# Ends of the expert stage in a fused Mamba and mixture-of-experts kernel: norms, splits and output groups in another order

## The reference

```python
def _layernorm(x, axis=-1, eps=1e-05):
    m = jnp.mean(x, axis=axis, keepdims=True)
    v = jnp.var(x, axis=axis, keepdims=True)
    return (x - m) / jnp.sqrt(v + eps)

# block 1: a Mamba block (norm, input projection, causal convolution of 4 taps, silu,
# step sizes by softplus, state scan over 1024 steps with 256 x 64 states, gate, projection)
x = _layernorm(x + mamba(x))

# block 2: four layers, each a mixture of 4 experts, the best 2 of 4 weighted
def _moe_layer(x, rw, rb, g, b, w1, b1, w2, b2):
    probs = softmax(x @ rw + rb); vals, idx = top_k(probs, 2); vals = vals / vals.sum()
    xhat = (x - mean) * rsqrt(var + EPS)
    xe = xhat[None] * g + b                      # per expert
    h = gelu(xe @ w1 + b1)                       # 128 -> 512, per expert
    y = h @ w2 + b2                              # 512 -> 128
    return sum over experts of comb * (x + y)    # comb: vals, zero for the two others
y = x
for l in range(4): y = _moe_layer(y, ...)
x = _layernorm(x + y)
```

## Time and profile before

| | |
|---|---|
| median of 3 runs | 2267.18 us |
| lowest, highest | 2264.71, 2272.36 us |
| the profiled execution, its own time | 2264.66 us |
| its span | 2262.8 us |
| PE, DVE, ACT, POOL busy | 95%, 81%, 71%, 42% of the span |
| expert stage | about 1386 to 2258 us of the span |

### The profile page before, as it was taken

The page is one execution under the profiler, slowest core; times in us unless marked ns, Lnnn a source line. Parts: engine busy times, 40 slices in busy tenths (PEclk is TensorE's granted clock), DMA queues, the critical chain, the costliest instruction groups (busy, mean ns, idle before and its releaser), DMA issues. The chain is left out here.

```text
span 2262.8 us, 50361 instructions
## 1 busy us (share of the span) xinstructions
PE 2139.4 (95%) x16960; PEld 1260.6 (56%) x16960; DVE 1841.2 (81%) x2779; ACT 1598.0 (71%) x2070; POOL 944.1 (42%) x452
## 2 busy tenths in 40 slices
PE   7887999999999999999999997999999999999997
PEld 3342333333333333333333335899999999999986
DVE  5768999999999999999999997565565566556665
ACT  4677988888888888888888884555455455544543
POOL 3225343434444443434343443544444444444442
PEclk9895999999999999999999999999999999999999
DMA  5887222222221212122221225100100010000000
GB/s 166 249 242 190 44 45 44 46 41 45 42 46 39 46 39 46 39 49 42 46 45 41 47 47 149 38 0 0 38 1 0 0 38 1 0 1 1 10 10 18
DMA packets 354957, 114.93 MB, mean 51 GB/s; under 512 B 283000, under 2 KB 345600, under 8 KB 354624
## 3 DMA queue, kind: packets, MB, share of 16 engines
q1 hardware_dynamic: 350416, 110.92, 20.0%
q10 hardware_dynamic: 4464, 3.02, 0.4%
HBM read 67.98 MB, written 45.88 MB: 50 GB/s over the span
## 5 line engine op out<-in xcount | busy, mean ns | idle before, releaser
L1518 DVE TENSOR_TENSOR_SCAN arena<-behind 128x1040 f32<-128x1040 f32 x512 | 1157.1, 2310 | 6.9 <-ACT behind L961 4.3
L1062 ACT ACTIVATE arena<-PS,arena 128x512 f32<-128x512 f32 x512 | 343.1, 689 | 395.7 <-PE PS L1294 395.4
L951 ACT ACTIVATE behind<-PS 128x1024 f32<-128x1024 f32 x512 | 527.3, 1030 | 133.7 <-DVE arena L1518 101.3
L1197 PE MATMUL PS<-arena 128*32 128x128 f32 x8192 | 565.9, 406 | 0.0
L961 ACT ACTIVATE behind<-PS 128x1024 f32<-128x1024 f32 x512 | 539.2, 1053 | 7.4 <-PE PS L1180 3.8
L1306 PEld LDWEIGHTS PS<-arena 128*128 128x128 f32 x4096 | 476.3, 193 | 7.9
L1306 PE MATMUL PS<-arena 128*128 128x128 f32 x4096 | 476.6, 276 | 0.0
L771 POOL COPY behind<-carry 128x64 f32<-128x64 f32 x128 | 209.3, 1635 | 517.2 <-DVE arena L1518 382.1
L1294 PE MATMUL PS<-parts_xh,parts_w 128*128 128x512 f32 x1536 | 383.6, 401 | 14.4 <-ACT arena L1062 13.6
L1197 PEld LDWEIGHTS PS<-arena 128*32 128x32 f32 x8192 | 234.6, 119 | 287.7 <-issue 210.5
L1180 PE MATMUL PS<-arena 96*128 96x512 bf16 x1024 | 314.4, 389 | 53.0 <-ACT behind L961 38.7
(11 more groups left out here) (131 smaller groups left out, 1413.1 us busy)
## 6 DMA issues: line engine op xcount, KB each, us to landing
dl_d<-arena SPq DMA_DIRECT2D x48, 256.0 KB, 3.0
du_d<-arena SPq DMA_DIRECT2D x48, 256.0 KB, 3.3
arena<-dl_d SPq DMA_DIRECT2D x512, 24.0 KB
arena<-b_d SPq DMA_DIRECT2D x64, 192.0 KB
arena<-du_d SPq DMA_DIRECT2D x512, 24.0 KB
b_d<-arena SPq DMA_DIRECT2D x48, 128.0 KB, 2.8
u_d<-behind SPq DMA_DIRECT2D x8, 512.0 KB, 4.1
sz_d<-arena SPq DMA_DIRECT2D x8, 512.0 KB, 4.8
```

What stands on the lines that cost most here:

```text
L951: nc.scalar.activation(seg(dA[:, half])[:, :, 1:], PS[:, 0:2, :].rearrange("p j (i t) -> p (j i) t", t=TC), ACT.Exp).then_inc(exp_done, 1)
L1062: nc.scalar.activation(hT[:, e % 2, c], PS[:, HIDDEN[(GT * e + c) % 3], :], ACT.Gelu, bias=bias1[:, lp, e * GT + c:e * GT + c + 1]).then_i ...
L1197: last = nc.tensor.matmul(PS[32 * j:32 * j + 32, 4 + kk, 0:DB], cd[:, pair, j, 32 * i:32 * i + 32], seg(hb[kk])[:, :, 1 + 16 * j + i], sta ...
L1518: nc.vector.tensor_tensor_scan(hb[kk][:, q * QD * SEG:(q + 1) * QD * SEG], dA[:, q % 2], dB[:, G_, lo:lo + QD * SEG], 0.0, ALU.mult, ALU.a ...
```

## The change

Five things are changed, all at the ends of the expert stage.

1. ACT makes the norm of group 0 ahead of the second copy of the last chunk's sums and ahead of the load of b2; both stood ahead of it.
2. In step 0 ACT makes the norm of group 1 ahead of the gelus of expert 2 (was: of expert 1) and the norm of group 2 ahead of those of expert 3 (was: of expert 2). PE transposes group 1 behind first 3 (was: behind second 0), and DVE splits group 1 behind the router of group 1 (was: behind the sum of expert 0).
3. In the last layer `finish` is parted: output sum and moments behind the sum of expert 0, the norm behind that of expert 1 (was: all of it ahead of the sum of expert 3). POOL makes its power ahead of the exponential (was: at the end of the step).
4. The last group's expert 3 is added and ended in two halves of two tiles. PE signals after half of the second products (`y_first`) and writes the other half to PSUM bank 5 instead of 7. POOL makes two powers of two tiles.
5. SP issues the last group's stores in two pairs, each behind its half, outside the loop.

```diff
+        def y_bank(n, e, s):
+            apart_from_first = isinstance(n, int) and n == NL * NG - 1 and e == E - 1 and s >= GT // 2
+            return 5 if apart_from_first else Y_BANK[e]
@@ sync
-            with sp.Fori(0, NG // 2) as g2:
+            with sp.Fori(0, NG // 2 - 1) as g2:
...
+            sp.wait_ge(f_fin, NG - 1 + FIN0)
+            for s in range(GT):
+                store_out(NG - 2, 0, s)
+            for s in range(GT):
+                sp.wait_ge(f_fin, NG + s // 2 + FIN0)
+                store_out(NG - 1, 1, s)
@@ gpsimd, step
                     stage_scores(n + 1, 0 if new else g + 1, new[0] if new else layer[0])
+                if isinstance(layer[0], int) and layer[0] == NL - 1 and not (isinstance(g, int) and g == 0):
+                    rsqrt(rs_o, o_var, o_rs, g)
                 if more:
                     stage_exp(n + 1)
                     stage_bias(n + 1, new[0] if new else layer[0], 1 - gp)
-                if isinstance(layer[0], int) and layer[0] == NL - 1 and not (isinstance(g, int) and g == 0):
-
-                    rsqrt(rs_o, o_var, o_rs, g)
 
             run_layers(pool, begin, step)
-            rsqrt(rs_o, o_var, o_rs, NG)
+            rsqrt(rs_o[:, 0:GT // 2], o_var, o_rs, NG)
+            rsqrt(rs_o[:, GT // 2:], o_var, o_rs, NG + 1)
@@ scalar
             evacuate(NC - 1, BP - 1, 0)
-            evacuate(NC - 1, BP - 1, 1)
-            act.dma_start(b2_s, b2.rearrange("p (l e h) -> p l e h", l=NL, e=E)).then_inc(b2_in, 16)
...
-                    if isinstance(n, int) and n == 0 and e == 1:
+                    begins = isinstance(n, int) and n == 0
+                    if begins and e == 2:
                         stage_norm(1, 1, 1)
-                    if more and e == 2:
+                    if more and e == (3 if begins else 2):
                         stage_norm(n + 2, (g + 2) % NG, gp)
...
-            run_layers(act, lambda first_layer: stage_norm(0, 0, 0), step)
+            def begin(first_layer):
+                stage_norm(0, 0, 0)
+                evacuate(NC - 1, BP - 1, 1)
+                act.dma_start(b2_s, b2.rearrange("p (l e h) -> p l e h", l=NL, e=E)).then_inc(b2_in, 16)
+            run_layers(act, begin, step)
@@ tensor, second
+                    if isinstance(n, int) and n == NL * NG - 1 and e == E - 1 and s == GT // 2 - 1:
+                        last.then_inc(y_first, 1)
@@ tensor, step
+                begins = isinstance(n, int) and n == 0
                 first(n, lp, gp, 1)
                 second(n, lp, 0)
-                if more:
+                if more and not begins:
                     stage_xh(n + 1, 1 - gp)
                 first(n, lp, gp, 2)
                 second(n, lp, 1)
                 first(n, lp, gp, 3)
+                if begins:
+                    stage_xh(1, 1)
                 second(n, lp, 2)
@@ vector
+            def finish_half(half):
+                g, n = NG - 1, NG * NL - 1
+                lo, hi = half * GT // 2, (half + 1) * GT // 2
+                if half == 0:
...
+                    dve.wait_ge(y_first, 1)
+                else:
+                    dve.wait_ge(f_y, FY0 + E * n + E)
+                for s in range(lo, hi):
+                    last = nc.vector.scalar_tensor_tensor(at(X, g, s), PS[:, y_bank(n, E - 1, s), s * P:(s + 1) * P],
+                                                          comb[:, 1, s * E + E - 1:s * E + E], at(X, g, s),
+                                                          ALU.mult, ALU.add)
...
+                nc.vector.tensor_tensor(xsum_o[:, lo:hi], tiles(X), tiles(X1), ALU.add).then_inc(f_fl, 1)
...
+                moments(f_fl, links + 1, lambda s: xsum_o[:, lo + s], st_o[:, lo:hi], mv_o[:, lo:hi], rs_o[:, lo:hi], GT // 2,
+                        o_var)
+            def finish_half_norm(half):
+                lo = half * GT // 2
+                dve.wait_ge(o_rs, NG + half)
+                scaled_apart(lambda s: xsum_o[:, lo + s], mv_o[:, lo:], rs_o[:, lo:], lambda s: xo[:, 1, lo + s], GT // 2
+                             ).then_inc(f_fin, 1)
@@ vector, step
                 add_expert(n, g, gp, 0)
+                if last_layer(l) and not (isinstance(g, int) and g == 0):
+                    finish_moments(g - 1)
                 if more:
-                    split_xh(n + 1, 1 - gp)
+                    if not begins:
+                        split_xh(n + 1, 1 - gp)
                     stage_scores(n + 1, next_l)
...
                 add_expert(n, g, gp, 1)
+                if last_layer(l) and not (isinstance(g, int) and g == 0):
+                    finish_norm(g - 1, 1 - gp)
                 if more:
                     stage_router(n + 1, 1 - gp)
+                if begins:
+                    split_xh(1, 1)
                 add_expert(n, g, gp, 2)
...
-                if last_layer(l) and not (isinstance(g, int) and g == 0):
-                    finish(g - 1, 1 - gp)
-                add_expert(n, g, gp, 3)
+                if not (last_layer(l) and isinstance(g, int) and g == NG - 1):
+                    add_expert(n, g, gp, 3)
 
             run_layers(dve, begin, step)
 
-            finish(NG - 1, 1)
+            finish_half(0)
+            finish_half(1)
+            finish_half_norm(0)
+            finish_half_norm(1)
```

More of the change, by code:

```diff
@@ L377, in build @@
         f_upper = sem("f_upper")
+        y_first = sem("y_first")
         f_neg = sem("f_neg")
@@ L661, in _, with store_out @@
                 load_weights(l)
[L663 removed]
+            def store_out(g, gp, s):
+                sp.dma_start(tokens(out, g * 2 + s // 2, s % 2), xo[:, gp, s, :]).then_inc(f_out[gp], 16)
+            with sp.Fori(0, NG // 2 - 1) as g2:
                 for gp in range(2):
@@ L1305, in second @@
                     for c in range(GT):
-                        last = nc.tensor.matmul(PS[:, Y_BANK[e], s * P:(s + 1) * P], hT[:, e % 2, c, s * P:(s + 1) * P],
+                        last = nc.tensor.matmul(PS[:, y_bank(n, e, s), s * P:(s + 1) * P], hT[:, e % 2, c, s * P:(s + 1) * P],
                                                 w2_s[lp][:, e * GT + c], start=(c == 0), stop=(c == GT - 1))
+                    if isinstance(n, int) and n == NL * NG - 1 and e == E - 1 and s == GT // 2 - 1:
+                        last.then_inc(y_first, 1)
                 last.then_inc(f_y, 1)
@@ L1697, in finish, with finish_norm @@
                 dve.wait_ge(f_fl, g * O_LINKS + 1)
+                moments(f_fl, g * O_LINKS + 1, lambda s: xsum_o[:, s], st_o, mv_o, rs_o, GT, o_var)
+            def finish_norm(g, gp):
                 dve.wait_ge(f_out[gp], 64 * (g // 2) + 64)
-                moments(f_fl, g * O_LINKS + 1, lambda s: xsum_o[:, s], st_o, mv_o, rs_o, GT, o_var)
                 dve.wait_ge(o_rs, g + 1)
                 scaled_apart(lambda s: xsum_o[:, s], mv_o, rs_o, lambda s: xo[:, gp, s], GT).then_inc(f_fin, 1)
+            def finish_half(half):
+                g, n = NG - 1, NG * NL - 1
+                lo, hi = half * GT // 2, (half + 1) * GT // 2
+                if half == 0:
+                    dve.wait_ge(x_in, 32)
+                    dve.wait_ge(f_fin, g + FIN0)
+                    dve.wait_ge(f_out[1], 64 * (g // 2) + 64)
+                    dve.wait_ge(f_x0, n + 2)
+                    dve.wait_ge(f_sum, FS0 + E * n + E - 1)
+                    dve.wait_ge(y_first, 1)
[5 more added lines that the diff above has]
+                                                          ALU.mult, ALU.add)
+                last.then_inc(f_last, 1)
+                dve.wait_ge(f_last, 3 + half)
+                links = g * O_LINKS + half * O_LINKS
+                tiles = lambda v: v[:, g * GT + lo:g * GT + hi, :]
+                nc.vector.tensor_tensor(xsum_o[:, lo:hi], tiles(X), tiles(X1), ALU.add).then_inc(f_fl, 1)
+                dve.wait_ge(f_fl, links + 1)
+                moments(f_fl, links + 1, lambda s: xsum_o[:, lo + s], st_o[:, lo:hi], mv_o[:, lo:hi], rs_o[:, lo:hi], GT // 2,
[5 more added lines that the diff above has]
+                             ).then_inc(f_fin, 1)
             def last_layer(l):
```

5 lines of the change are left out of this document (2 added, 3 removed).

## The result

The kernel after took 2250.34 us (median of 6 runs, 2246.17 to 2253.39), the kernel before beside it 2265.78 us (median of 6, 2264.71 to 2272.36): a ratio of 0.9926, with a 95% interval of 0.9908 to 0.9944. The profiled execution took 2247.83 us, its span is 2246.2 us, 16.6 less than before. PE is busy 2135.7 us of it, 3.7 less than in the earlier trace rows; the rest of the 16.6 us was idle time of PE and the tail behind it.

What follows compares the result with a forecast made beforehand. PE, busy 95% of the span, was taken as the bound, leaving its stalls and the tail: 6.8 + 5.5 + 4.5 = 16.8 us off gives 2247.8 for the profiled execution, forecast 2249 (chance 0.68), range 2243.5 to 2256.5.

Steps and rivals of the forecast that it cites:

- Start of the stage: Step 0 of the expert stage: earlier norms let group 1 start at 1426.1 instead of 1432.86, 6.8 us gained.
- (a): Group 0's start: ACT's norm ahead of the last copy lets the transposes start at the sums' end, 3.2 us gained.
- (b): DVE and POOL chain in step 0: POOL's product stays, a held DVE norm limits the chain's shift to 2.75 us.
- (c): PE in step 0: one gelu wait of 6 us and one low-clock stretch costing 2.5; PE done at 1424.4.
- (d): Group 1's release: its split now stands behind router 1, so PE starts at 1426.1, 1.7 us after its own bound.
- Last layer: Shorter DVE and POOL ring: no PE stalls, 25.69 us a group, 5.5 us gained, with 2.8 us of slack counted.
- Rival 2: Last layer keeps its stalls because split and scores stand behind the output moments on DVE; time 2254.5, chance 0.11.
- Tail: After PE's end: halved last sum and norm, earlier paired stores; last store at 2255.95 against 2260.46, 4.5 us gained.
- the step of 1.2 from the execution to the median: End of the sum: from 2247.8 for the profiled execution to 2249, halfway to the earlier median's 2.5 us excess.
- Rival 3: Step 0: PE's longer idle, 6 us against 3.94, leaves the clock low for long; time 2273, chance 0.04.
- Rival 4: Tail: halves do nothing because stores set the end, 3.4 for 4.5 us; inside the forecast's range, no separate chance.
- The scatter: Ends of layers: one to three low-clock dips of 1.6 us each, either way, not in the sum.

Runs made afterwards that it cites:

- start_only: Kernel after with parts 3 to 5 taken back, so only the start of the stage is changed; 2257.59 us, 0.9969 of the kernel before.
- norm0_only: Part 1 alone: group 0's norm is early, norms of groups 1 and 2 and group 1's transposes and split in old places; 2261.81 us, 0.9986.
- split_early: Kernel after with group 1's split moved ahead of its router on DVE; 2247.02 us, 0.9916 of the kernel before.
- layer_only: Part 3 alone: only the last layer is changed, the last group is ended whole; 2256.97 us, 0.9973 of the kernel before.
- tail_only: Parts 4 and 5 alone: last group in halves and paired stores, group 6's norm still ahead of the last sum; 2264.07 us, 0.9996 of the kernel before.
- bias_parts: exp_early with each layer's piece of 32 one-column bias matmuls cut into two of 16; 2239.97 us, against 2244.5 us for the baseline beside it.
- exp_early: split_early with POOL making the first router's exponential ahead of the powers for chunk 31 and group 1; 2244.48 us, 0.9904 of the kernel before.
- exp_early2: exp_early unchanged, run once more as the baseline beside bias_parts; 2244.5 us, 0.9903 of the kernel before.

## Why the prediction was right

**Start of the stage: predicted 6.8, measured 6.5 in the profile after, 6.8 in start_only.** (a) The transposes without a wait, 3.2: as predicted. At group 1 norm0_only gives 3.0 for it, 2.3 by the chain and 0.7 by the clock, where the prediction had 2.75 by the chain alone. (b) The chain through DVE and POOL: the held norm of chunk 30 came as named (2.40 us). The reduction started at 1391.31 and not at 1390.3, but because the first load of X, behind which DVE's moments stand, landed 1.0 us later in this execution (1380.45 above, 1379.47 below), so that POOL's product started at 1386.43 and not at 1385.45; that is also the part by which the router's end (1425.4, predicted 1424.5) and group 1 (1426.86, predicted 1426.1) are late. The row of the kernel before:

```profile
1379.47 0.87 DVE L1355 BATCH_NORM_STATS2 arena<-arena 128x6 f32<-128x128 f32 x4 [0.84 <-DMA arena<-x_d]
```

(c) One wait in step 0, predicted 6, measured 6.59, and one low stretch: from PE's return to the end of the second products predicted 11.0 us, measured 10.4, since the low clock cost 1.9 and not 2.5. (d) Router and split set group 1's start, and split_early shows that this wait was the new bound: without it group 1 starts 2.2 us earlier. Bounding (d) by PE's own time was right, and the bound was reachable by one more move of the split.

**Last layer: predicted 5.5, measured 5.55.** 25.69 us a group, no wait for a gelu. The first sum started 9.39 us after the group (predicted 9.3). One thing the count left out: the output sum, 0.68 us where it is free, is mostly held beside POOL's product (five of seven; median 1.33, longest 2.33 us). It cost nothing, since the slack of 2.8 us in the count covered it. Rival 2 is excluded by layer_only.

**Tail: predicted 4.5, measured 5.05.** The mechanism held; the sum was 0.5 too small. The first store is issued 3.2 us after PE's end (predicted 3.6, most of the difference because SP issues it 0.02 us behind DVE's norm, and 0.27 behind it in the kernel before). A store outside the loop follows the one ahead of it in 0.62 us (four in 2.47), which I had at 0.73; I had named 0.57 as the upper bound of 5.0, and three steps of 0.11 are 0.3 us. Against that, the span ends 2.58 us behind the start of the last store and not 2.34. POOL's power for two tiles takes 0.70 us and not the 1.01 of four, but nothing waits for that: the last norm ends at 2242.69, ahead of the third store at 2243.02. What I did not say is how the gain depends on the last layer's part: "DVE is free then (the norm of group 6 is long done)" is true only with part 3, and tail_only measures what the same edit is worth without it, 1.1 us.

**Sum: predicted 16.8, measured 16.6**; the profiled execution 2247.8, measured 2247.83. That it fits this closely is luck: counted from the sums' end the three parts gave 17.1, 0.3 less at the start and 0.55 more in the tail than predicted, and the 0.5 by which the sums ended later took the excess away. The forecast of 2249.0 is 1.3 under the median of 2250.34. The term that is too small here is the step of 1.2 from the execution to the median. For the kernel before it fits (2265.78, the median of the six runs beside the result, is 1.1 over the profiled execution); for the kernel after it is 2.5. Three of the six runs after took 2252.8 to 2253.4 us, three 2246.2 to 2247.8, and layer_only and the kernel after once more show such pairs too. The kernel before has single runs that high as well (2272.36, 2270.37 and 2270.14), so the upper level is not made by the change, though it came more often with it. All the profiles of the kernel after fell on the lower level, so the cause of the upper one, some 6 us, stays open.

**Rival 3**, a clock that stays low after the longer idle, did not come: one low stretch, the block of 64 second products in 8.10 us against 7.30. **Rival 4** did not come either; the stores follow the halves.

**The scatter** named at 1.6 us a dip was right in size, and its cause, which the prediction did not know, is the whole piece of narrow matmuls, as far as bias_parts shows. I took it as noise against which everything shifts; it was 4.8 us that could be had.

## What to carry to other kernels

Ends of a pipelined stage are worth a list of their own: for each wait there, ask which moved instruction makes the engine late and where its inputs are ready, and test the parts alone, since two parts can be worth more together (here 5.05 against 3.0 us) than apart. On a side engine with two jobs ready, put first the one on which the long chain hangs: an exponential ahead of a power was worth 2.5 us. Where matmuls of one column stand in one long piece, cut the piece and put wide matmuls between; look for it where PE is 100% busy and the granted clock still is not 1.00. Read the block behind a shortened idle time, too: in exp_early the first three matmuls were fast and the 64 behind them were not.

## What the runs showed of the hardware

- 32 one-column matmuls in a row (3.63 us) were followed at 24 of 33 layer ends (eleven traces, two or three of three in each) by a granted clock at the lower level, though PE was never idle; cut into twice 16 (1.84 us each) with 12 matmuls of 512 columns between, at none of three.
- Behind PE's idle times of 2.42, 2.78 and 2.90 us in step 0 (exp_early, bias_parts, exp_early2) the next three matmuls took 0.97 to 1.03 us, and then the granted clock fell: the 64 behind them took 8.94, 8.94 and 8.51 us instead of 7.30. Behind idle times of 3.9 us and more in step 0 the clock was low at once: 1.65 us for three, in all traces here. Behind the 3.22 us of the kernel before it was not low (1.00 from 1384 to 1392 us).
- A DVE instruction with its operands in SBUF that started beside POOL's product ended only behind POOL's end: 0.08 to 0.15 us behind it in three forms of 128x128 (2.40, 2.15 and 3.45 us where 0.2 to 0.35 is the free time), 0.55 us behind it in five output sums of 128x512. With one operand in PSUM it did not wait: 161 additions of an expert's output in the kernel after started beside one of POOL's two products and took 0.34 us each (median; longest 0.35), as the 347 others did.
- Stores issued in unrolled code follow each other in 0.62 us, from a loop in 0.73.
